# A gated cross-attention and expert layer: the low parts of transposed rows move from VectorE to TensorE and ScalarE, and VectorE masks more score banks

## The reference

```python
x = x + tanh(g_x) * attn(layernorm(x), ctx)     # q, k, v with biases; scores / sqrt(8)
    scores = where(causal | padding, -inf, scores); w = softmax(scores)
    out = (w @ v) @ Wo.T + bo
x = x + tanh(g_f) * moe(layernorm(x))           # softmax router, top 2 of 16,
    h = silu(x @ gate) * (x @ up); out = sum_e combine_e * (h @ down)
```

## Time and profile before

| | |
|---|---|
| median of 3 runs | 240.3 us (240.22 to 240.74) |
| the profiled execution's own time | 240.54 us |
| its span, first to last instruction | 238.7 us |
| PE busy | 218.6 us (92%), 1259 matmuls |
| DVE busy | 175.5 us (74%) |
| ACT busy | 96.4 us (40%) |
| POOL busy | 94.8 us (40%) |
| granted TensorE clock | 1.00 throughout |

### The profile page before, as it was taken

The page is one execution under the profiler, slowest core; times in us unless marked ns, Lnnn a source line. Parts: engine busy times, 40 slices in busy tenths (PEclk is TensorE's granted clock), DMA queues, the critical chain, the costliest instruction groups (busy, mean ns, idle before and its releaser), DMA issues.

```text
span 238.7 us, 3921 instructions
## 1 busy us (share of the span) xinstructions
PE 218.6 (92%) x1259; PEld 158.4 (66%) x1259; DVE 175.5 (74%) x495; ACT 96.4 (40%) x190; POOL 94.8 (40%) x127
## 2 busy tenths in 40 slices
PE   0798798989999999999999899999999899999993
PEld 0675554554565554556456778888898798988892
DVE  2577978748898989886733778569975887775665
ACT  2357257756676766756667120121212112111110
POOL 6239335400528494945301021308996263320000
PEclk9999999999999999999999999999999999999999
DMA  6472220007861202021104100042544323112105
GB/s 184 106 237 58 67 66 22 4 0 154 178 155 45 46 23 61 8 66 30 40 10 129 47 0 0 6 166 54 148 131 128 126 88 90 45 55 80 44 0 176
DMA packets 26275, 18.33 MB, mean 77 GB/s; under 512 B 15600, under 2 KB 22320, under 8 KB 26256
## 3 DMA queue, kind: packets, MB, share of 16 engines
q1 hardware_dynamic: 25952, 17.87, 27.3%
q10 hardware_dynamic: 304, 0.22, 0.4%
HBM read 14.15 MB, written 1.11 MB: 64 GB/s over the span
## 4 chain that ended last, share of the span: by engine, by line
PE 65%; DVE 10%; POOL 7%; ACT 6%; DMA 5%; issue 3%; SPq 2%; ACTq 0%; DVEq 0%; POOLq 0%
PE bank L1031 57%; DMA wkv_n<-in_L_xattn_Wv 2%; PE bank L1071 2%; DVE mneg L891 2%; POOL cT L556 2%; ACT q L621 2%; PE bank L1091 2%; POOL w_d L560 2%; POOL cT L555 2%; POOL w_d L559 1%; SPq L437 1%; DMA w_t<-comb_d 1%; DVE pT L959 1%; DVE x_sb L1024 1%; ACT pT L701 1%
## 5 line engine op out<-in xcount | busy, mean ns | idle before, releaser
L1031 PE MATMUL bank<-xT,cT 128*128 128x512 f32 x288 | 70.6, 393 | 1.0 <-DVE pT L951 0.7
L1031 PEld LDWEIGHTS bank<-xT,cT 128*128 128x128 f32 x288 | 52.5, 188 | 12.4 <-issue 1.2
L688 ACT ACTIVATE pT<-bank 128x512 f32<-128x512 f32 x24 | 14.4, 599 | 78.5 <-PE bank L1031 78.5
L701 ACT ACTIVATE pT<-bank 128x512 f32<-128x512 f32 x64 | 38.0, 599 | 17.9 <-PE bank L1031 16.6
L1031 PE MATMUL bank<-w_d,q 128*128 128x256 f32 x288 | 38.6, 284 | 1.7 <-issue 0.9
L1031 PEld LDWEIGHTS bank<-w_d,q 128*128 128x128 f32 x288 | 37.0, 190 | 4.6 <-issue 3.2
L1031 PE MATMUL bank<-q,kz 112*128 112x512 f32 x64 | 37.5, 586 | 0.0
L891 DVE TENSOR_REDUCE mneg<-bank 128x4 f32<-128x512 f32 x44 | 29.2, 683 | 3.1 <-PE bank L1031 2.6
L951 DVE TENSOR_TENSOR pT<-pT,bank 128x512 f32<-128x512 f32 x24 | 16.4, 685 | 17.0 <-PE bank L1031 15.2
L1031 PE MATMUL bank<-kz,q 96*128 96x512 f32 x64 | 26.3, 418 | 2.4 <-DVE mneg L891 1.8
L1031 PE MATMUL bank<-ident_b,cmask 128*128 128x512 bf16 x64 | 24.6, 384 | 1.3 <-ACT pT L701 0.6
(11 more groups left out here) (129 smaller groups left out, 292.0 us busy)
## 6 DMA issues: line engine op xcount, KB each, us to landing
w_t<-comb_d SPq DMA_DIRECT2D x16, 192.0 KB, 2.7
w_t<-comb_d SPq DMA_DIRECT2D x16, 128.0 KB, 2.8
padf<-in_L_ffn_down_w SPq DMA_DIRECT2D x12, 128.0 KB, 2.2
c_sb<-in_ctx SPq DMA_DIRECT2D x2, 512.0 KB, 6.5
q<-cT SPq DMA_DIRECT2D x8, 128.0 KB, 2.4
w_t<-comb_d SPq DMA_DIRECT2D x16, 64.0 KB, 2.7
out<-x_sb SPq DMA_DIRECT2D x4, 256.0 KB, 2.4
c_sb<-in_L_ffn_gate_w SPq DMA_DIRECT2D x8, 96.0 KB, 2.1
```

The source lines that it names most:

```text
L688: nc.scalar.activation(act_g[:, n % 2], bank[0][:], ACT.Silu).then_inc(a_ok, 1)
L701: nc.scalar.activation(pT[:, i // 4, i % 4, :], bank[2 + s % 2][:], ACT.Exp, scale=SCALE).then_inc(p_done, 1)
L1031: return nc.tensor.matmul(dst, a, b, start=start, stop=stop, skip_group_check=True)
```

## The change

Three edits. `added_by_reduction` now holds for all n from 16 to 55, so 20 more banks are left bare and masked by DVE's four fused instructions; `masked` gets two buffers. For the jobs AT and YT of batches 0 to 6 DVE's subtraction is gone: one slot after the job, right behind `scores_k`, PE waits for ACT's high part and adds minus identity times the high part onto the transposed rows in the same bank, and ACT copies the bank to the low part behind that slot's exponential. `emptied` of these 14 jobs is ACT's copy. The transposes are written as matmuls with `is_transpose` of which only the first starts the accumulation. POOL makes the negative identity at the start. Waits on `pool_init` are raised by one where they stand for the same steps; those lines are left out here.

```diff
--- before.py
+++ after.py
@@ -104,6 +104,7 @@
         cst = sb("cst", [P, C_N])
         ident = cst[:, C_ID:C_ID + P]
         ident_b = sb("ident_b", [P, P], BF16)
+        ident_w = sb("ident_w", [P, QR + P], F32R)
         x_sb = sb("x_sb", [P, NB, D])
         xb_sb = sb("xb_sb", [P, NB, D])
         c_sb = sb("c_sb", [P, NB, D])
@@ -182,7 +183,7 @@
         comb_t = sb("comb_t", [E, NT])
         c_rep = w_t[:, 0:CR * TH].bitcast(F32).rearrange("p (s n) -> p s n", s=CR)
         zero = sb("zero", [P, 1])
-        masked = sb("masked", [P, 4, L])
+        masked = sb("masked", [P, 2, 4, L])
 
 
         def gu_view(t, flat):
@@ -231,6 +232,8 @@
         job_lo = sem("job_lo")
         q_lo = sem("q_lo")
         k_ok = sem("k_ok")
+        row_sub = sem("row_sub")
+        row_lo = sem("row_lo")
         v_ok = sem("v_ok")
         mt_ok = sem("mt_ok")
         s_done = sem("s_done")
@@ -303,10 +306,14 @@
                 hn[j] = count
                 count += {"kv": 2}.get(j[0], 1)
 
-        ln = {j: n for n, j in enumerate(j for j in JOBS if j[0] not in ("MT", "q", "kv"))}
+        SUB_SLOT = {(k, b): AT_SLOT[k, b] + 1 for k in ("AT", "YT") for b in range(NB - 1)}
+        ROWS = sorted(SUB_SLOT, key=lambda j: SUB_SLOT[j])
+        ln = {j: n for n, j in enumerate(j for j in JOBS if j not in SUB_SLOT and j[0] not in ("MT", "q", "kv"))}
 
         def emptied(j):
 
+            if j in SUB_SLOT:
+                return row_lo, ROWS.index(j) + 1
             if j[0] == "MT":
                 return mt_ok, j[1] + 1
             if j[0] == "q":
@@ -328,7 +335,7 @@
 
         def added_by_reduction(n):
 
-            return bool(n % 2 and 2 * G <= n < CH - G)
+            return bool(2 * G <= n < CH - G)
 
         def issued(s):
 
@@ -501,6 +508,7 @@
             for sub in range(2):
                 pool.memset(vz[:, :, sub::2, 16 * sub + HD:16 * sub + HD + 1], 1.0)
             pool.memset(mt[:].bitcast(F32), 0.0)
+            pool.tensor_scalar(ident_w[:, QR:QR + P], ident, -1.0, None, ALU.mult).then_inc(pool_init, 1)
             pool.tensor_copy(ident_b[:], ident).then_inc(pool_init, 1)
 
             def separate_keys(b):
@@ -669,6 +677,12 @@
                     high(j)
             high(("MT", 0))
 
+            def row_low(j):
+
+                sc.wait_ge(row_sub, ROWS.index(j) + 1)
+                dst = aT[1][:] if j[0] == "AT" else xT[1][:, :, toks(j[1])]
+                nc.scalar.copy(dst, jbank(j)[:, 0:D].rearrange("p (c q) -> p c q", c=DC)).then_inc(row_lo, 1)
+
             def copy_o(b):
 
                 sc.wait_ge(pv_done, 2 * b + 2)
@@ -700,6 +714,9 @@
                         sc.wait_ge(pv_done, 2 * (b - 1) + i // 4 + 1)
                     nc.scalar.activation(pT[:, i // 4, i % 4, :], bank[2 + s % 2][:], ACT.Exp,
                                          scale=SCALE).then_inc(p_done, 1)
+                for j in ROWS:
+                    if s == SUB_SLOT[j]:
+                        row_low(j)
                 if s == SILU_SLOT[0]:
                     silu(0)
                 if s % G == 1 and G < s < CH + G:
...
@@ -884,7 +901,7 @@
                 if added_by_reduction(n):
                     ve.wait_ge(max_ok, n - 1)
                     for g in range(4):
-                        ins = nc.vector.tensor_tensor_reduce(masked[:, g], bank[SQ_BANK[n % 3]][:, g * L:(g + 1) * L], cmask[:, n // G],
+                        ins = nc.vector.tensor_tensor_reduce(masked[:, n % 2, g], bank[SQ_BANK[n % 3]][:, g * L:(g + 1) * L], cmask[:, n // G],
                                                              -1.0, 4.0 * BIG, ALU.add, ALU.min, mneg[:, r, 4 * hf + g:4 * hf + g + 1])
                     ins.then_inc(max_ok, 1)
                     return
...
@@ -989,13 +1006,13 @@
                     nc.vector.tensor_scalar(xn[:, NB - 1], x_sb[:, NB - 1], mv[:, NB - 1, 0:1], rstd[:, NB - 1:NB],
                                             ALU.subtract, ALU.mult).then_inc(xn_last, 1)
                 if s == 20:
-                    ve.wait_ge(pool_init, 4)
+                    ve.wait_ge(pool_init, 5)
                     ve.wait_ge(d_rw, 16)
                     own(nc.vector.tensor_copy(rw[0][:, :, 0:E], rw_n[:]))
                     settle()
                     nc.vector.tensor_tensor(rw[1][:, :, 0:E], rw_n[:], rw[0][:, :, 0:E].bitcast(F32), ALU.subtract).then_inc(rw_ok, 1)
                 for j in takes_at(s):
-                    if j[0] != "MT":
+                    if j[0] != "MT" and j not in SUB_SLOT:
                         take(j)
                 for n, at in WEIGH_SLOT.items():
                     if s == at:
@@ -1038,6 +1055,19 @@
                     for k, (a, b) in enumerate(terms):
                         last = mm(dst, a(c), b(c), first and c == 0 and k == 0, c == chunks - 1 and k == 2)
                 return last
+
+            def transpose_rows(ps, rows):
+
+                for c in range(DC):
+                    ins = nc.tensor.matmul(ps[:, c * L:(c + 1) * L], rows[:, c * P:(c + 1) * P], ident,
+                                           start=c == 0, stop=True, is_transpose=True, skip_group_check=True)
+                return ins
+
+            def subtract_rows(j):
+
+                pe.wait_ge(job_hi, hn[j] + 1)
+                hi = aT[0][:] if j[0] == "AT" else xT[0][:, :, toks(j[1])]
+                mm(jbank(j)[:, 0:D].rearrange("p (c q) -> p c q", c=DC), ident_w[:, QR:QR + P], hi, False, True).then_inc(row_sub, 1)
 
             def job(j):
                 if before(j) is not None:
@@ -1092,8 +1122,7 @@
                 elif k == "AT":
                     pe.wait_ge(*emptied(("TO", j[1])))
                     a = an[:].rearrange("p g r d -> p (g r d)")
-                    for c in range(DC):
-                        ins = nc.tensor.transpose(ps[:, c * L:(c + 1) * L], a[:, c * P:(c + 1) * P], ident)
+                    ins = transpose_rows(ps, a)
                 elif k == "WO":
                     pe.wait_ge(*emptied(("AT", j[1])))
                     ins = three(ps[:, 0:D], [lambda c, i=i: aT[i][:, c] for i in range(2)],
@@ -1103,8 +1132,7 @@
                         pe.wait_ge(xn_last, 1)
                     else:
                         pe.wait_ge(xn_ok, 1 + TPH + j[1] + 1)
-                    for c in range(DC):
-                        ins = nc.tensor.transpose(ps[:, c * L:(c + 1) * L], xn[:, j[1], c * P:(c + 1) * P], ident)
+                    ins = transpose_rows(ps, xn[:, j[1]])
                 elif k == "SC":
                     pe.wait_ge(*emptied(("YT", (j[1] + 1) * TPH - 1)))
                     pe.wait_ge(rw_ok, 1)
...
@@ -1218,6 +1246,9 @@
             for s in range(SLOTS):
                 if s < CH:
                     scores_k(s)
+                for j in ROWS:
+                    if s == SUB_SLOT[j]:
+                        subtract_rows(j)
                 for n in ahead(s):
                     scores_q(n)
                 if s % G == 5 and s < CH:
```

More of the change, by code:

```diff
@@ L806, in take @@
                 elif k == "vn":
-                    ve.wait_ge(pool_init, 3)
+                    ve.wait_ge(pool_init, 4)
                     for sub in range(2):
@@ L1208, in _ @@
             pe.wait_ge(mask_ok, 1)
-            pe.wait_ge(pool_init, 3)
+            pe.wait_ge(pool_init, 4)
             pe.wait_ge(*emptied(("bias",)))
```

## The result

| | before | after |
|---|---|---|
| median | 240.26 us (240.01 to 240.74, 4 runs) | 244.44 us (244.30 to 244.64, 4 runs) |
| span of the profiled execution | 238.7 us | 242.6 us |
| its own time | 240.54 us | 244.43 us |

A forecast was written before the change was run, and what follows sets the result against it. TensorE and VectorE were both nearly full, so instruction order and the last wait in each slot decide. Batch terms 0.7 + 0.7 + 0.16 + 0.7 + 1.04 + 1.05 = 4.35 gave 244.9 us profiled, 244.7 median; range 242.5 to 246.8.

The forecast's parts named there:

- i = 2 and i = 6: Slots with these numbers modulo 8: ScalarE's copy or casts end last, so a mask less on TensorE gives nothing.
- i = 0 and i = 4: Slots with these numbers modulo 8: TensorE has nothing to wait for, so each mask less saves 0.24 us.
- 0.32 + 0.11: YT's subtraction in slot 36: 0.32 us TensorE standstill for ScalarE's high part plus 0.11 of work, 0.43 together.
- "about 0.3" and "about 0.55": Trace sign: TensorE idle ahead of the subtractions, 12 times about 0.3 us and about 0.55 at two of them.
- no more than the 0.15: At the subtraction: result-to-reading-matmul latency of 0.15 us limits the weight load's extra; otherwise up to 0.1 more each.
- took off 0.15: Slots 41 to 48: two subtractions cost 0.84 us, less 0.15, making +0.7.
- ScalarE's low copy: Slots 52 and 60: YT's low-part copy delays AT's high part, so AT's subtraction costs 0.54 + 0.11 us.
- The projection of batch 0: Slot 15: WO waits for AT's low copy behind casts and exponential, starting at 61.0 to 61.1; +1.1 to +1.2 us.
- late by 0.25: Around slots 11 and 12: VectorE is the late engine, and one fused bank there adds 0.25 us.
- VectorE stands between MT and its time: Trace sign at MT, the transpose of the maxima: if VectorE held it up, the prediction counted itself wrong.
- the covered waits: Subtractions reach TensorE after the high part is ready, so masks pay: 239.4 or 237.0 us; chance 0.08.
- VectorE's pace: VectorE's casts fall under GpSimd's instructions, delaying the maxima, 0.4 us in each of four batches: 246.4 us; chance 0.13.

The follow-up runs named there:

- the masks put back: Changed kernel with 8 of the 20 new bare banks (n = 26, 30, ... 54) given their mask matmul back on TensorE: 244.52 us, ratio 1.0179.
- mask edit alone: Kernel before with all 40 banks n = 16 to 55 masked by VectorE, low parts still by VectorE's subtraction: 238.93 us, ratio 0.9949.
- the run without the wait: Changed kernel, TensorE's subtraction reading a constant operand without waiting for the high part, low parts left as full rows: 240.93 us, ratio 1.0031.
- the last batch's banks: Kernel before with VectorE masking n = 16 to 63, 48 banks in all, low parts as before: 238.02 us, ratio 0.9904.
- subtractions moved: Changed kernel with TensorE's subtraction behind scores_q instead of ahead of it in its slot: 242.95 us, ratio 1.0120.

## Why the prediction was right

The working was a count of slot lengths, so each term can be held against the table of starts.

| slots | predicted | measured |
|---|---|---|
| 8 to 16 | +0.7 | +0.69 |
| 17 to 32 | +0.72 | +0.69 |
| 33 to 40 | +0.16 | +0.13 |
| 41 to 48 | +0.70 | +0.82 |
| 49 to 56 | +1.04 | +0.94 |
| 57 to 62, to the start of 63 | +1.05 | +0.94 |
| start, up to slot 8 | 0 | -0.32 |
| behind slot 63 | 0 | 0 |

- **Masks.** Right: nothing in i = 2 and i = 6 (the masks put back), 0.23 to 0.25 us in i = 0 and i = 4 (mask edit alone, slots 20, 24, 28, 32, 36 and 40). In the first batches they gave 0.24 in slot 8, 0.25 in 10, 0.23 in 16.
- **The wait.** The estimate 0.32 + 0.11 for YT in slot 36 against 1.34 - 1.15 + 0.24 = 0.43. Its parts were divided wrongly: TensorE's next matmul comes 0.66 + 0.22 after the slot's start, where I had 0.75 + 0.11. From the end of the high part to the subtraction pass 0.05 us and not 0.14, and the subtraction takes 0.22 behind its wait and not 0.11. The two errors of 0.1 us cancel, which is luck. For the same reason the idle times up to the subtraction are smaller than the "about 0.3" and "about 0.55" forecast for the trace: 0.19 to 0.23 us in ten slots and 0.33 in slots 53 and 61. The sentence that the weights leave room for no more than the 0.15 doesn't hold: behind a wait a subtraction takes 0.1 us more than without one, and its weight load stands behind the wait with it (89.53 both). The Trainium skill's rule that a matmul may begin before its weights are in (TensorE: Matmul & The Clock Gate, section on the array of 32 x 32 parts) may still hold, but it doesn't make the load free here. That the price of the subtractions is mostly waiting is shown by the run without the wait: 3.5 us, against 1.4 for their matmuls.
- **41 to 48.** I took off 0.15 for time that MT had lost to VectorE. In slot 45 of the kernel before the values start at 100.87 and MT at 101.88, the 1.00 that they take where nothing holds MT, so there was nothing to regain.
- **49 to 62.** The mis-sized term is ScalarE's low copy, counted as 0.4 in the queue. The two copies behind the exponential start 0.25 us apart (115.17 and 115.42): 0.15 too much in each pair, which covers the difference of 0.1.
- **The projection of batch 0.** Right in mechanism, 60.52 for 61.05, of which 0.3 us is the earlier start of this execution. Alone it is worth 1.05 us.
- **VectorE.** Hidden where the working said so: in slots 21, 29, 37 and 45 of the changed kernel MT starts 1.00 us behind the weighted values. Its busy time in the batch's window grew by 0.23 us, 10.14 to 10.37. It is not hidden in slots 11 to 13, where the working had it late by 0.25: slots 12 and 13 are 0.32 longer together, and MT waits 1.00 us for it where it waited 0.48. So the sign "VectorE stands between MT and its time" did show, in this one slot, at about the price that the sum had for it. With the last batch's banks it held MT in slot 45 also, by a cast of 1.30 us of the kind of the earlier trace rows. In all twelve traces, a cast that began while a 128 x 512 instruction of GpSimd still had 0.1 us or more to run ended 0.03 to 0.05 us behind that instruction's end, and one that began ahead of it took 0.18 us. In slot 29 of the mask edit alone the cast comes first by 0.01 us, and VectorE's next instruction takes the delay:

```profile
77.14 0.18 DVE L901 CAST mt<-mneg 128x32 fp32r<-128x32 f32 x1
77.15 1.32 POOL L556 TENSOR_TENSOR cT<-c_sb,cT 128x512 fp32r<-128x512 f32 x1
77.36 1.15 DVE L903 TENSOR_TENSOR mt<-mneg,mt 128x32 fp32r<-128x32 f32 x1
```

That agrees with the exclusive lock of which the Trainium skill tells (SBUF — State Buffer, section on the two separate sides). It makes the cast's time a matter of what GpSimd does just then: in the mask edit alone it took 0.18 and 0.19 us at slots 29 and 37, where it had taken 0.95 and 1.16 before. In slot 37 MT came 0.2 us sooner behind the weighted values than before, and that slot got 0.19 shorter.
- **The start.** The profiled execution of the changed kernel reached slot 0 at 29.77 us, 0.32 before the other. Over the twelve traces of this study slot 0 begins between 29.62 and 30.15, and the 30.15 is the changed kernel with its subtractions moved, so I take it for no effect of the change. Without it the sum is 4.2 us, which is also the difference of the medians, where I had 4.35.

The rivals: the covered waits are refuted by the run without the wait, since then it would have changed nothing. VectorE's pace as the cause of the loss is refuted by the mask edit alone, which is faster than the kernel before although VectorE holds TensorE in slots 13 and 30.

## What to carry to other kernels

To move a step between two full engines is to add handovers, and their latency weighs more than the work: here 0.12 us of matmul cost 0.43. Before a wait is placed in an in-order queue, count what stands between it and the release, and put it behind work that doesn't need it; one matmul more in between (two where a mask stood there) was worth 1.5 us over eight waits. Work taken off the busiest engine pays only in the slots where that engine ends last: about half of the 20 masks gave nothing, and the others were worth having alone.

## What the runs showed of the hardware

- A 256-column matmul with its own weights took TensorE 0.12 us from start to the next start when nothing held it, and 0.22 us right behind a semaphore wait, where its weight load of 0.19 us starts with it instead of 0.22 us ahead. The idle time counted up to its start understates the wait by the same 0.1 us.
- Two copies of 128 x 256 behind an exponential on ScalarE start 0.25 us apart when the second's input is there, though each row says 0.37 to 0.39.
- VectorE's 128 x 32 cast took 0.18 us alone or when it began ahead of GpSimd's 128 x 512 instruction, and up to 1.30 us, until 0.03 to 0.05 us behind that instruction's end, when it began after it. Which it was changed from kernel to kernel: at slot 36 it took 1.08 us in the changed kernel and 0.18 with the subtractions moved.
